# The down projection of a chain of conditioned residual blocks: whole-array matmuls, gamma and beta on two halves of the partitions, and a copy on ScalarE

## The reference

```python
def _L2_cond_ref(hidden_states, conditions, down_project, down_gamma, ...):
    dg = conditions @ down_gamma
    db = conditions @ down_beta
    ...
    w_down = down_project[None, :, :] * dg[:, None, :] + db[:, None, :]
    down = jnp.einsum('bsd,bdh->bsh', hidden_states, w_down)
    act = jax.nn.relu(down)
    w_up = up_project[None, :, :] * ug[:, None, :] + ub[:, None, :]
    up = jnp.einsum('bsh,bhd->bsd', act, w_up)
    return up + hidden_states
```

## Time and profile before

| what | value |
| --- | --- |
| time, median of 3 runs | 523.35 us (523.15 to 528.42) |
| time of the profiled execution | 525.21 us |
| its span in the trace | 523.4 us |
| TensorE matmul busy | 486.2 us, 93% |
| TensorE weight loads busy | 352.9 us, 67% |
| VectorE busy | 405.8 us, 78% |
| GpSimd busy | 390.7 us, 75% |
| ScalarE busy | 333.7 us, 64% |

### The profile page before, as it was taken

One profiled execution on the slowest core, in us unless ns is written; L12 is line 12 of the kernel. 1 busy time (PEld: TensorE's weight loads), 2 busy tenths in 40 slices (PEclk: granted clock), 3 DMA queues, 4 the chain that ended last, 5 costly groups with the idle time before them and its releaser, 6 DMA issues.

```text
span 523.4 us, 9425 instructions
## 1 busy us (share of the span) xinstructions
PE 486.2 (93%) x3198; PEld 352.9 (67%) x3198; DVE 405.8 (78%) x696; ACT 333.7 (64%) x638; POOL 390.7 (75%) x367
## 2 busy tenths in 40 slices
PE   2987887999999999999999999999999999998993
PEld 2953643757677676767676767677676768687682
DVE  2858876858888787879787878788787978887763
ACT  4674667356667575767775758667576767666832
POOL 6468799888877879697878787788878693787321
PEclk9999999999999999999999999999999999999997
DMA  8788705625252161608081616244352614104102
GB/s 305 233 299 213 201 20 123 162 80 126 82 125 81 49 197 44 201 2 241 2 214 31 187 58 164 81 87 158 81 165 49 190 35 98 49 11 153 40 2 80
DMA packets 34989, 61.78 MB, mean 118 GB/s; under 512 B 5017, under 2 KB 17413, under 8 KB 34580
## 3 DMA queue, kind: packets, MB, share of 16 engines
q1 hardware_dynamic: 28756, 43.98, 29.9%
q0 software_dynamic: 5344, 16.87, 11.1%
q10 hardware_dynamic: 864, 0.61, 0.4%
HBM read 52.58 MB, written 8.87 MB: 117 GB/s over the span
## 4 chain that ended last, share of the span: by engine, by line
PE 68%; DVE 16%; issue 4%; POOL 4%; DMA 4%; ACT 1%; DVEq 0%; SPq 0%; POOLq 0%; ACTq 0%
PE ps_d L948 10%; PE ps_c L902 10%; PE ps_c L904 9%; PE ps_c L903 9%; PE ps_a L976 5%; PE ps_d L962 5%; DVE ps_d L1361 3%; DVE ps_d L1352 3%; PE ps_a L994 3%; DVE x_t L1367 3%; PE ps_b L935 3%; DVE tm_t_l L1437 3%; PE ps_a L988 3%; DMA set_wdec<-in_nets_rows 2%; DMA set_wdec<-in_W_dec 1%
## 5 line engine op out<-in xcount | busy, mean ns | idle before, releaser
L1507 POOL DMA_INDIRECT pw_rows<-in_pw,gidx x64 | 64.0, 1000 | 17.8 <-issue 17.7
L948 PE MATMUL ps_d<-xm_t,l_w 128*128 128x512 f32 x128 | 58.9, 603 | 2.2 <-POOL xm_t L1516 2.2
L1209 ACT ACTIVATE h<-h,nb_h,rstd_h 128x256 f32<-128x256 f32 x64 | 33.3, 591 | 34.6 <-POOL nb_h L1531 34.6
L1516 POOL TENSOR_TENSOR xm_t<-x_t,style 128x1024 f32<-128x1024 f32 x16 | 30.5, 1906 | 21.9 <-DVE x_t L1345 21.2
L1546 POOL TENSOR_TENSOR h<-xhat,pw_rows 128x1024 f32<-128x1024 f32 x16 | 38.0, 2378 | 7.5 <-ACT xhat L1209 7.1
L948 PEld LDWEIGHTS ps_d<-xm_t,l_w 128*128 128x128 f32 x128 | 23.1, 190 | 26.8 <-issue 24.2
L1565 POOL TENSOR_TENSOR w_up<-up_rep,ugub 128x1024 f32<-128x1024 f32 x16 | 37.9, 2370 | 2.2 <-issue 2.0
L1240 ACT ACTIVATE tm_t_h<-ps_a 128x1024 fp32r<-128x1024 f32 x16 | 16.4, 1027 | 36.1 <-DVE ps_a L1413 36.1
L1551 POOL TENSOR_TENSOR h<-h,pw_rows 128x1024 f32<-128x1024 f32 x16 | 38.2, 2390 | 1.3
L1567 POOL TENSOR_TENSOR w_up<-w_up,ugub 128x1024 f32<-128x1024 f32 x16 | 38.2, 2385 | 1.3
L902 PE MATMUL ps_b<-w_h,act_t_l 128*128 128x256 f32 x128 | 37.7, 295 | 0.4 <-DVE act_t_l L1450 0.4
(11 more groups left out here) (251 smaller groups left out, 1558.8 us busy)
## 6 DMA issues: line engine op xcount, KB each, us to landing
ugub<-ugub_scratch SPq DMA_DIRECT2D x32, 512.0 KB
x_t<-in_x_t SPq DMA_DIRECT2D x16, 512.0 KB
out<-y_out SPq DMA_DIRECT2D x15, 512.0 KB
set_wdec<-in_W_dec SPq DMA_DIRECT2D x2, 1920.0 KB, 9.6
set_wdec<-in_int_W SPq DMA_DIRECT2D x1, 1536.0 KB, 9.8
set_wdec<-in_nets_rows SPq DMA_DIRECT2D x1, 1152.0 KB, 12.5
pw_rows<-in_pw,gidx POOLq DMA_INDIRECT x64
set_wdec<-in_nets_W SPq DMA_DIRECT2D x1, 768.0 KB, 4.9
```

The costliest lines, as they stand in the source:

```text
L948: m = eng.matmul(ps_l1[:, o, :], l1_w[:, k, o * P:(o + 1) * P], xm_t[:, k, :], start=k == 0, stop=k == KB - 1)
L1209: m = eng.activation(out[:, j, :], src[:, j, :], ACT.Identity, bias=nb[k][:, j:j + 1], scale=rstd[k][:, j:j + 1])
L1507: eng.indirect_dma_start(pw_rows[c.ring][:, j, :], None, t["pw"], bass.IndirectOffsetOnAxis(ap=gidx[c.ring][:, j:j + 1], axis=0)).then_inc ...
```

## The change

The down projection is done with the whole array: 2 matmuls of 128 columns and 512 rows for a chunk, so that gamma's product lies on partitions 0 to 63 and beta's on 64 to 127. The table `dgdb` is laid out in the same way, and takes one copy in place of four when it is made. `v_dnmul` becomes one product of 128 by 512. A new stage `act_dnv` on ScalarE copies beta's half from partitions 64 to 127 of `ps_dn` to partitions 0 to 63 of `dn_v`, and `v_dnadd` adds the two on 64 partitions by 512 elements. `dn` is the same buffer as `dn_v`. In VectorE's order `v_tmlow` now stands ahead of `v_dnadd` in the loop and in the drain (not in the warm-up); in ScalarE's order of the loop `act_ysquare` stands between `act_dnv` and `act_relu`, and in the drain `act_dnv` stands right ahead of `act_relu`. Two semaphores of the second block's stages become one that is counted twice for each chunk.

```diff
 def pe_dn:
-            x = x2_t[:, :, :].rearrange("p k (j e s) -> p k e j s", e=2, s=S)
-            for part in range(2):
-                for k in range(KB):
-                    for e in range(2):
-                        m = eng.matmul(ps_dn[e * HID:(e + 1) * HID, part * CT * S:(part + 1) * CT * S],
-                                       down_w[:, k, part * HID:(part + 1) * HID], x[:, k, e],
-                                       start=k == 0, stop=k == KB - 1)
+            for k in range(KB):
+                m = eng.matmul(ps_dn, down_w[:, k, :], x2_t[:, k, :], start=k == 0, stop=k == KB - 1)
             m.then_inc(p_dn, 1)
...
+        def act_dnv(eng, c):
+            wait(eng, v_dnu, c.n + 1)
+            eng.activation(dn_v[:, :], ps_dn[HID:P], ACT.Copy).then_inc(a_dnv, 1)
...
 def act_relu:
             for e in range(2):
                 rows = slice(e * HID, (e + 1) * HID)
-                m = eng.activation(act_dn[rows, :, e, :], dn[rows, :].rearrange("p (j s) -> p j s", s=S), ACT.Relu)
+                src = dn[:, :].rearrange("p (j e s) -> p e j s", e=2, s=S)
+                m = eng.activation(act_dn[rows, :, e, :], src[:, e], ACT.Relu)
...
 def v_dnmul:
-            d = ps_dn.rearrange("p (k j s) -> p k j s", k=KB, s=S)
-            tab = dgdb[:, :, bass.ds(c.n * CT, CT)].unsqueeze(3).broadcast_to([P, KB, CT, S])
-            wait(eng, v_dn, c.n)
-            eng.tensor_tensor(d[:, 0], d[:, 0], tab[:, 0], ALU.mult)
-            eng.tensor_tensor(dn_v[:, :].rearrange("p (j s) -> p j s", s=S), d[:, 1], tab[:, 1], ALU.mult).then_inc(v_dnu, 1)
+            d = ps_dn.rearrange("p (b s) -> p b s", s=S)
+            tab = dgdb[:, bass.ds(c.n * CB, CB)].unsqueeze(2).broadcast_to([P, CB, S])
+            eng.tensor_tensor(d, d, tab, ALU.mult).then_inc(v_dnu, 1)
 def v_dnadd:
-            eng.wait_ge(v_dnu, c.n + 1)
-            wait(eng, a_relu, c.n)
-            eng.tensor_tensor(dn[:, :], ps_dn[:, 0:CT * S], dn_v[:, :], ALU.add).then_inc(v_dn, 1)
+            wait(eng, a_dnv, c.n + 1)
+            eng.tensor_tensor(dn[:, :], ps_dn[0:HID], dn_v[:, :], ALU.add).then_inc(v_dn, 1)
...
 def act_dg:
-            for k in range(KB):
-                for e in range(2):
-                    src = ps_b[k * HID:(k + 1) * HID, 0, 2 * P:3 * P].rearrange("h (n e) -> h e n", e=2)
-                    m = eng.activation(dgdb[e * HID:(e + 1) * HID, k, :], src[:, e, :], ACT.Copy)
-            m.then_inc(c_dg, 1)
+            eng.activation(dgdb[:, :], ps_b[:, 0, 2 * P:3 * P], ACT.Copy).then_inc(c_dg, 1)
...
 VectorE, order:
-                             (v_x2add, 3), (v_hlow, 5), (v_tmprod, 5), (v_dnmul, 3), (v_dnadd, 3), (v_tmlow, 5),
+                             (v_x2add, 3), (v_hlow, 5), (v_tmprod, 5), (v_dnmul, 3), (v_tmlow, 5), (v_dnadd, 3),
```

More of the change, by code:

```diff
@@ L194, in conditioned_residuals @@
         x2_t = x1_t
-        dn_v = sb("dn_v", [P, CT * S])
-        dn = sb("dn", [P, CT * S])
+        dn_v = sb("dn_v", [HID, CH])
+        dn = dn_v
         y_sq = sb("y_sq", [P, CT, D], BF16)
@@ L304, in conditioned_residuals @@
             sem("p_" + n) for n in "t x1 l1 dn up x3r xht tm ms hht cp w1x w1t w1m w1 w2".split())
-        (a_u, a_th1, a_th, a_relu, a_x3, a_x3h, a_xhat, a_xht, a_tmh, a_msh, a_hhat, a_hh, a_silu, a_silh, a_sq, a_oh, a_ysq, a_gidx) = (
-            sem("a_" + n) for n in "u th1 th relu x3 x3h xhat xht tmh msh hhat hh silu silh sq oh ysq gidx".split())
-        (v_x1, v_l1u, v_l1v, v_x2, v_dnu, v_dn, v_x3t, v_x3l, v_bnx, v_mvx, v_tm, v_tml, v_ms, v_msl,
+        (a_u, a_th1, a_th, a_dnv, a_relu, a_x3, a_x3h, a_xhat, a_xht, a_tmh, a_msh, a_hhat, a_hh, a_silu, a_silh, a_sq, a_oh, a_ysq, a_gidx) = (
+            sem("a_" + n) for n in "u th1 th dnv relu x3 x3h xhat xht tmh msh hhat hh silu silh sq oh ysq gidx".split())
+        (v_x1, v_l1, v_x2, v_dnu, v_dn, v_x3t, v_x3l, v_bnx, v_mvx, v_tm, v_tml, v_ms, v_msl,
          v_bnh, v_mvh, v_h, v_hl, v_sill, v_y1, v_y) = (
             sem("v_" + n) for n in
-            "x1 l1u l1v x2 dnu dn x3t x3l bnx mvx tm tml ms msl bnh mvh h hl sill y1 y".split())
+            "x1 l1 x2 dnu dn x3t x3l bnx mvx tm tml ms msl bnh mvh h hl sill y1 y".split())
         g_xm, g_vex, g_rx, g_nbx, g_h1m, g_h1, g_veh, g_rh, g_nbh, g_upm, g_up, g_x3be, g_vey, g_ry = (
@@ L1358, in v_l1min @@
                 eng.wait_ge(d_bias, 16)
[L1359 removed]
+            eng.wait_ge(v_l1, 2 * c.n + 1)
             for k in range(KB):
                 m = eng.tensor_scalar(ps_l1[:, k, :], ps_l1[:, k, :], l1_b[:, k:k + 1], CLAMP, ALU.add, ALU.min)
[L1362 removed]
+            m.then_inc(v_l1, 1)
         def v_x2add(eng, c):
[L1366 removed]
+            eng.wait_ge(v_l1, 2 * c.n + 2)
             eng.scalar_tensor_tensor(x2_t[:, :, :], ps_l1[:, :, :], -CLAMP, x1_t[:, :, :],
@@ L1668, in _ @@
                            (act_th1, 15), (act_x3, 13), (act_xnorm, 13), (act_hh, 12), (act_tmh, 12),
-                           (act_relu, 14), (act_x3h, 13), (act_ysquare, 11), (act_msh, 12), (act_xht, 13),
+                           (act_dnv, 14), (act_relu, 14), (act_x3h, 13), (act_ysquare, 11), (act_msh, 12), (act_xht, 13),
                            (act_onehot, 13), (act_th2, 15), (act_hnorm, 13), (act_silu, 12), (act_silh, 12),
                            (act_x3, 14), (act_xnorm, 14), (act_hh, 13), (act_onehot, 14), (act_tmh, 13),
-                           (act_relu, 15), (act_x3h, 14), (act_xht, 14), (act_msh, 13), (act_ysquare, 12),
+                           (act_dnv, 15), (act_relu, 15), (act_x3h, 14), (act_xht, 14), (act_msh, 13), (act_ysquare, 12),
                            (act_hnorm, 14), (act_sil0, 13), (act_sil1, 13), (act_hh, 14), (act_x3, 15),
```

25 lines of the change are left out of this document (11 added, 14 removed).

## The result

The changed kernel takes 541.42 us, the median of 7 runs (538.89 to 548.07); the kernel before, run beside it on the same chip, takes 527.15 us (523.15 to 528.42, 7 runs). The ratio of the two is 1.0293, with a 95% interval of 1.0255 to 1.0332: slower by 2.6% to 3.3%. (The two medians alone divide to 1.027.) The forecast of 13.4 us over 523.35 is 2.56%, at the lower edge of that interval; the measured 2.93% is 15.3 us, 538.7 us on 523.35. The level, 541.42, is 4.6 us above the forecast of 536.8, outside the 534.5 to 539 that stood for it and inside the 531 to 542 that takes in two rivals; 3.8 of that is the kernel before, which ran at 527.15 and not at 523.35 beside it.

The account below looks back on a forecast made before the run. TensorE's matmuls were taken as the bound. Loop waits of 10.6 us, drain 1.1 and warm-up 1.9, less 0.2 for shorter matmuls in other chunks, gave +13.4 us: 523.35 to 536.8 us, range 531 to 542.

Parts of the forecast that it names:

- two rivals: The alternatives rival (a), 533 us, chance 0.11, and Rival (b), 541 us, chance 0.10.
- Part 2: Loop: the ms gains wait for the later down-projection sum; 0.94 us a round, 10.6 us over eleven rounds.
- rival (a): Sum on 64 partitions costs 0.42 us, not 0.70; each of eleven rounds loses 0.28 less: 533 us, chance 0.11.
- Part 1: Down projection's matmuls on TensorE: four whole-array records take 1.77 us instead of 1.88, gaining 0.11 us a chunk.
- Part 3: ScalarE's queue ahead of the up projection in the loop: later copy of `xh_t` costs nothing, 0.3 us left.
- Rival (b): ScalarE's queue makes the up projection wait too, 0.4 us more in each of eleven rounds: 541 us, chance 0.10.
- Part 4: First round behind the loop's order: up projection waits for the late `xh_t` copy; 1.2 us, less 0.11.
- Part 5: Warm-up: the open chain from down projection to up projection lengthens, 0.85 us twice and some 0.2; 1.9 us.
- Rival (e): TensorE's gaps of 1.4 us in each round might lower the granted clock; no size given, chance 0.02.
- rival (d): Dropping packing makes the down projection take 3.8 us, by the skill's factor of two: 569 us, chance 0.01.

Follow-up runs that it names:

- the order alone: Kernel before with only VectorE's tm low half moved ahead of the down projection's sum, in loop and drain: 536.77 us, ratio 1.0243.
- the two runs on orders: Kernel before with tm's low half ahead of the sum, 536.77 us; the same plus ScalarE's relu behind the squares of y, 534.13 us.
- the second profile: Changed kernel run again unaltered, for another profile: 539.82 us, ratio 1.0321 to the kernel before.

## What the prediction had right, and the step that failed

**Part 2, the wait, was right.** I forecast the end of the sum at 4.60 after the first tm matmul, the gains at 4.65 and the transposes at 5.09; they were at 4.57, 4.63 and 5.07. The sum took 0.67 us, forecast 0.70, so rival (a) is out, and the two products of 64 partitions show why. That the place of the sum makes the wait is shown twice: the order alone costs 1.11 us a round (0.77 when the relu stands behind the squares), and with the gains waiting for the product instead the round falls by 0.74.

**The count was off by one round, and hidden by luck.** I had eleven stalls at 0.94 to 1.0 us, 10.6 in all. The runs show ten rounds at 1.06, also 10.6, and an eleventh stall that cost nothing, since the round ahead of chunk 3 had idle time. Two misses that cancel.

**Part 1 was the wrong sign.** "The new stage has 4 records: 1.77 us. Gain 0.11 us a chunk." It took 1.91, a loss of 0.03. The step that failed is the row it was taken from: `pe_l1` is followed by whole-array matmuls, the down stage by strips of 24 rows, and the last record before them costs 0.59 and not 0.44. Over ten rounds that is 1.4 us; with it, 0.94 becomes 1.08.

**Part 3 was right.** The copy of `xh_t` ends at 8.48 (forecast 8.51), the up projection starts at 8.74 with 0.26 left (forecast 0.3). Rival (b) did not happen, but the two runs on orders show how near it was: with the relu in its old place it costs 0.3 a round.

**Part 4** forecast 1.09 (its own rows give nearer 1.0: 439.3 against 438.24, less 0.11) and nothing for the round after; measured 0.97 and 0.17.

**Part 5 is the step that failed: it put the clock at nothing.** The chain was right: its two waits grew by 0.83 each (forecast 0.85) and the third chunk by 0.23 (forecast 0.2). But the warm-up was given 1.9 us and took 3.4 (0.83 + 2.34 + 0.23). The rest is the granted clock, which went to 0.50 at 55 us, right behind waits of 1.40 and 2.04: the 16 matmuls of one up projection took 3.48 us and not 2.02, 1.46 us more. Rival (e) was the place for it, and was given 0.02 and no price, because "in the warm-up, from 60 to 90 us, TensorE is busy 25.76 of 30 us and the clock is 1.00". That is the stretch behind the one that matters. With the idle time filled, the stretch from chunk 0 to chunk 1 is 1.6 us shorter in the profile, and the median 2.1 us lower, which is less than the 1% that a time can tell. How much of the 1.46 is the change's stays open, since the clock also fell once in the warm-up of the kernel before.

**The sum.** Forecast 13.4; the spans with the setup evened out give 14.8, which is 13.3 and the clock's 1.46. On 523.35 that is 538.2, against 538.7 by the ratio. That the changed kernel's level was 541.42 also has a part that is not of the change: the kernel before ran at 527.15 beside it and at 523.3 to 525.7 beside the others. Its own runs move with the clock as well: beside the second profile, 522.79 to 524.57 us at a mean granted clock of 0.995, and 527.78 at 0.988.

**The factor of two.** The Trainium skill, page TensorEngine Tiling (Array Packing), section Overview, has packing as up to twice as fast where a dimension is 64 or less. The packed form with the same rows takes 1.87 us and the whole array 1.91, so here, with all 128 columns in use either way, there is nothing to win or lose by it: rival (d) is out. The same page, section Tiling Modes, says that a switch of mode drains the engine; the trace agrees that something is lost there, 0.09 us where strips of 24 rows follow, and doesn't show that it is a drain.

## What to carry to other kernels

Where an engine is the bound, ask for each wait how early its releaser is now: here the sum had 0.52 us, and both the change's form and its order used it up. Take the price of a stage from a row with the same neighbour behind it, not only with the same shape. And where TensorE already waits much, a wait can cost more than its length, because the clock falls; look at the granted clock in that stretch, and not in the mean or in the stretch behind. Before two times are compared, look in both traces for what the change doesn't touch: one late table of the setup was worth 4 us and more here.
